# Message passing over edges: operands of the second loop's products moved from SBUF to PSUM

## What is computed

```
e0 = feat0[edge_src];  e1 = feat1[edge_src]
ea0 = edge_attr[:, :1];  ea1 = edge_attr[:, 1:4]
h = gelu(edge_scalar_attr @ W_mlp1 / sqrt(8));  h = gelu(h @ W_mlp2 / sqrt(64))
w00, w01, w10, w11 = h @ Wp_00, h @ Wp_01, h @ Wp_10, h @ Wp_11
out0_a = w00 * e0 * ea0
out0_b = w11 * sum(e1 * ea1, over 3 components) / sqrt(3)
out1_a = (w01 * e0) x ea1          # 32 x 3
out1_b = w10 * e1 * ea0            # 32 x 3
n0, n1 = segment_sum of [out0_a, out0_b], [out1_a, out1_b] by edge_dst
```

## Time and profile before

| | us |
|---|---|
| time, median of 3 runs | 5811.78 (5809.79 to 5824.05) |
| the profiled execution's own time | 5874.45 |
| its span from first to last instruction | 5872.5 |
| busy in the span: PE / DVE / ACT / POOL | 3935.2 / 3079.9 / 1722.9 / 3442.4 |
| mean granted TensorE clock, share of full speed | 0.796 |

### The profile page before, as it was taken

The page is one execution under the profiler, slowest core; times in us unless marked ns, Lnnn a source line. Parts: engine busy times, 40 slices in busy tenths (PEclk is TensorE's granted clock), DMA queues, the critical chain, the costliest instruction groups (busy, mean ns, idle before and its releaser), DMA issues. The chain is left out here.

```text
span 5872.5 us, 85330 instructions
## 1 busy us (share of the span) xinstructions
PE 3935.2 (67%) x14958; PEld 2602.4 (44%) x14958; DVE 3079.9 (52%) x9402; ACT 1722.9 (29%) x5039; POOL 3442.4 (59%) x3340
## 2 busy tenths in 40 slices
PE   5566666667666666666675777767677676686667
PEld 3233434444333434334453554445455454454445
DVE  3333443444433444434595666666676565675566
ACT  1233333333333333333531222222222121222222
POOL 3455555555555555555275577667677676666663
PEclk6777778877877778877897787878888787887788
DMA  5333433333333333333212111111111111111111
GB/s 162 103 103 101 106 105 102 105 103 104 103 101 99 104 100 105 102 102 106 60 34 62 40 44 43 42 43 44 44 42 43 42 43 42 43 42 42 43 43 38
DMA packets 395187, 430.87 MB, mean 73 GB/s; under 512 B 194933, under 2 KB 286713, under 8 KB 394763
## 3 DMA queue, kind: packets, MB, share of 16 engines
q0 software_dynamic: 103168, 211.49, 13.8%
q1 hardware_dynamic: 290294, 214.04, 13.6%
q10 hardware_dynamic: 1428, 2.71, 0.2%
HBM read 411.12 MB, written 16.78 MB: 73 GB/s over the span
## 5 line engine op out<-in xcount | busy, mean ns | idle before, releaser
L1105 POOL DMA_INDIRECT conv_rows<-feat,conv_idx x1612 | 1780.2, 1104 | 892.7 <-issue 545.1
L160 POOL DMA_INDIRECT ring_rows<-xl,ring_idx x1612 | 1524.8, 946 | 1323.8 <-DVE attn_msg L730 750.8
L589 PE MATMUL attn_sums_ps<-attn_msg,attn_onehot 128*128 128x136 f32 x3224 | 584.4, 337 | 857.3 <-ACT attn_onehot L630 402.5
L1121 PE MATMUL conv_sums_ps<-conv_vals,conv_onehot 128*128 128x256 f32 x3224 | 932.7, 439 | 146.8 <-issue 80.3
L589 PEld LDWEIGHTS attn_sums_ps<-attn_msg,attn_onehot 128*128 128x128 f32 x3224 | 515.7, 236 | 899.6 <-issue 461.2
L1128 PE MATMUL conv_w_ps<-c_Wp,conv_hid 128*128 128x256 f32 x1612 | 508.5, 445 | 548.2 <-ACT conv_hid L1158 278.2
L1152 ACT ACTIVATE conv_scaled<-conv_w_ps,conv_edge 128x64 f32<-128x64 f32 x1612 | 374.7, 315 | 1701.9 <-remote 804.5
L1121 PEld LDWEIGHTS conv_sums_ps<-conv_vals,conv_onehot 128*128 128x128 f32 x3224 | 660.8, 216 | 407.6 <-issue 295.3
L736 DVE TENSOR_TENSOR attn_leaky<-attn_pre_ps,attn_fifth 128x512 f32<-128x512 f32 x403 | 276.9, 687 | 979.4 <-issue 498.5
L623 ACT ACTIVATE attn_fifth<-attn_pre_ps 128x512 f32<-128x512 f32 x403 | 238.4, 592 | 1620.2 <-remote 1110.5
L1128 PEld LDWEIGHTS conv_w_ps<-c_Wp,conv_hid 128*128 128x128 f32 x1612 | 350.5, 224 | 648.4 <-ACT conv_hid L1158 302.6
(11 more groups left out here) (169 smaller groups left out, 4674.7 us busy)
## 6 DMA issues: line engine op xcount, KB each, us to landing
c_xT<-in_attrT SPq DMA_DIRECT2D x403, 256.0 KB
attn_rel<-rel_group SPq DMA_DIRECT2D x403, 126.0 KB
ring_rows<-xl,ring_idx POOLq DMA_INDIRECT x1612
conv_rows<-feat,conv_idx POOLq DMA_INDIRECT x1612
conv_radial<-in_radialT SPq DMA_DIRECT2D x806, 8.0 KB
attn_xr_win<-xr_parts SPq DMA_DIRECT2D x403, 31.5 KB
attn_limit<-limit SPq DMA_DIRECT2D x403, 16.0 KB
conv_idx<-in_src_tiles SPq DMA_DIRECT2D x403, 2.0 KB
```

Source lines behind the costliest of these rows:

```text
L160: pool.indirect_dma_start(self.rows[:, b, t, :], None, self.q["xl"][:, :], bass.IndirectOffsetOnAxis(ap=self.idx[:, s.slot(2), j * TG + t: ...
L589: last = nc.tensor.matmul(to, onehot[:, g.slot(2), t, :], msg[:, g.slot(2), t, :, :].rearrange("p h o -> p (h o)"), start=wins > 1 or t == ...
L1105: pool.indirect_dma_start(rows[:, k.slot(NX), t, :], None, q["feat"][:, :], bass.IndirectOffsetOnAxis(ap=idx[b][:, t:t + 1], axis=0)).then ...
L1121: last = nc.tensor.matmul(to, onehot[:, g.slot(2), t, :], vals[:, g.slot(2), t, :], start=wins > 1 or t == 0, stop=wins > 1 or t == TG - 1)
```

## The change

`scaled` is gone: ACT writes the scaled weights over the weights in `w_ps`, in PSUM. The componentwise products `dots` lie in a bank of PSUM. The three components of the edge's vector are copied by ACT, for each group, to `edge3` in PSUM (12 elements per partition, one buffer), behind a wait for `vals_ready` of the group before, and DVE waits for that copy. One `reduce_sum` over the three components takes the place of two additions. Every DVE operation of the eight (now seven) thus reads at most one tensor from SBUF.

```diff
-        scaled = tile("scaled", [P, 2, TG, 2 * MUL])
-        dots = tile("dots", [P, TG, 3, MUL])
-        dot = tile("dot", [P, 2, TG, MUL])
+        dot = tile("dot", [P, TG, MUL])
...
+        dots = bank("dots_ps", [P, TG, 3, MUL])
+        edge3 = bank("edge3_ps", [P, TG, 3])
+        edge3_ready = sem("edge3_ready")
...
-        PRODUCTS = 5
+        PRODUCTS = 4
...
                     act.wait_ge(w_ready, g.uses())
-                    at_least(act, vals_ready, g.back(2).uses())
                     for t in range(TG):
-                        nc.scalar.activation(scaled[:, g.slot(2), t, :], w_ps[:, g.slot(2), t, 0:2 * MUL], ACT.Copy,
+                        here = w_ps[:, g.slot(2), t, 0:2 * MUL]
+                        nc.scalar.activation(here, here, ACT.Copy,
                                              scale=edge4[:, bass.ds(g.index(TG, t), 1), 0:1].rearrange("p t c -> p (t c)")).then_inc(scaled_ready, 1)
+                    at_least(act, vals_ready, g.back(1).uses())
+                    nc.scalar.activation(edge3[:, :, :], edge4[:, bass.ds(g.index(TG), TG), 1:4], ACT.Copy).then_inc(edge3_ready, 1)
...
-                        a1 = bc(edge4[:, bass.ds(g.index(TG), TG), 1:4], 3, MUL)
+                        a1 = bc(edge3[:, :, :], 3, MUL)
                         to, w = vals[:, s, :, :], w_ps[:, s, :, :]
                         at_least(dve, vals_ready, g.back(1).uses())
+                        dve.wait_ge(edge3_ready, g.uses())
                         dve.wait_ge(rows_gathered[g.slot(NX)], g.uses(NX, 16 * TG))
                         nc.vector.tensor_tensor(dots[:, :, :, :], e1, a1, ALU.mult).then_inc(products, 1)
                         dve.wait_ge(scaled_ready, g.uses(1, TG))
                         nc.vector.tensor_tensor(scal[:, :, :], w[:, :, 2 * MUL:3 * MUL], e0, ALU.mult).then_inc(products, 1)
+                        nc.vector.tensor_tensor(to[:, :, 0:MUL], w[:, :, 0:MUL], e0, ALU.mult)
                         dve.wait_ge(products, g.index(PRODUCTS, 1))
-                        nc.vector.tensor_tensor(dot[:, 0, :, :], dots[:, :, 0, :], dots[:, :, 1, :], ALU.add).then_inc(products, 1)
-                        nc.vector.tensor_tensor(to[:, :, 0:MUL], scaled[:, s, :, 0:MUL], e0, ALU.mult)
+                        nc.vector.reduce_sum(dot[:, :, :], dots[:, :, :, :].rearrange("p t c w -> p t w c"), mybir.AxisListType.X).then_inc(products, 1)
+                        nc.vector.tensor_tensor(to[:, :, MUL:D].rearrange("p t (c w) -> p t c w", c=3), e1, bc(w[:, :, MUL:2 * MUL], 2, 3), ALU.mult)
+                        dve.wait_ge(products, g.index(PRODUCTS, 2))
+                        nc.vector.tensor_tensor(to[:, :, D:D + V3].rearrange("p t (c w) -> p t c w", c=3), bc(scal[:, :, :], 2, 3), a1, ALU.mult).then_inc(products, 1)
                         dve.wait_ge(products, g.index(PRODUCTS, 3))
-                        nc.vector.tensor_tensor(dot[:, 1, :, :], dot[:, 0, :, :], dots[:, :, 2, :], ALU.add).then_inc(products, 1)
-                        nc.vector.tensor_tensor(to[:, :, MUL:D].rearrange("p t (c w) -> p t c w", c=3), e1, bc(scaled[:, s, :, MUL:2 * MUL], 2, 3), ALU.mult)
-                        nc.vector.tensor_tensor(to[:, :, D:D + V3].rearrange("p t (c w) -> p t c w", c=3), bc(scal[:, :, :], 2, 3), a1, ALU.mult).then_inc(products, 1)
-                        dve.wait_ge(products, g.index(PRODUCTS, 4))
-                        nc.vector.tensor_tensor(to[:, :, D + V3:DX], dot[:, 1, :, :], w[:, :, 3 * MUL:4 * MUL], ALU.mult).then_inc(vals_ready, 1)
+                        nc.vector.tensor_tensor(to[:, :, D + V3:DX], dot[:, :, :], w[:, :, 3 * MUL:4 * MUL], ALU.mult).then_inc(vals_ready, 1)
```

## The result

| | median of its runs | lowest to highest | profiled execution | mean clock granted there |
|---|---|---|---|---|
| before | 5829.51 us (6 runs) | 5809.79 to 5843.61 | 5874.45 us | 0.796 |
| after | 5944.26 us (6 runs) | 5932.32 to 5966.89 | 5959.12 us | 0.791 |

The change makes the kernel 2.0% slower: ratio 1.0203, 95% interval 1.0177 to 1.0229. The forecast of no change (5812 us, with 5700 to 5920 as its own range) missed. The time lies where the rival "the first loop's rhythm" put it (5902 to 5982, about 5940 us, with a chance of 0.19), and inside the wide range of 5500 to 5990.

The account below looks back on a forecast made before the run. The second loop's pace was put at 6.56 us per group, with held-up gathers and POOL's pauses trading off rather than POOL's work binding. Gathers, DVE and ACT each added 0: 5874 us profiled, 5812 by the median, range 5500 to 5990.

Parts of the forecast that it names:

- The forecast of no change: Whole kernel: freed held-up time returns as POOL pauses, so 5812 us, own range 5700 to 5920, chance 0.52.
- the first loop's rhythm: Rival, second loop: without held-up gathers, pauses rise to 1.8 to 2.0 us per group; about 5940 us, chance 0.19.
- Gathers are held up by reads of two SBUF tensors: Second loop: gathers stand still while DVE reads two SBUF tensors, 0.64 us per group, 258 us at most.
- What takes their place: Second loop: POOL's pauses grow by the 0.64 us freed, keeping held-up time plus pauses at 1.58 us per group.
- POOL's idle time: Ahead of second-loop gathers: a rise of about 250 us would be the sign of the forecast.
- Windows: Second loop: the forecast fails if windows of 316 us hold more than 205 or fewer than 183 gathers.
- Quick stretches: Second loop: stretches at 4 us per group would be gone, a sign listed for the forecast.
- VectorE: Second loop: two additions go, one reduction comes, +0.07 us per group; +28 us if DVE were the bound, counted as nothing.
- Operands in PSUM: DVE's second-loop operations: 2 to 8 ns on six operations, 5 to 20 us in 403 groups, counted as nothing.
- ACT's copy: Second loop: 12-element copy and its wait, 0.2 us per group, hidden behind other work; up to +242 us if uncovered.

Follow-up runs that it names:

- e6: Kernel after with one useless 384-element product more per group on VectorE, reading two SBUF tensors: 5930.86 us, 1.019 of the kernel before.
- e3: Kernel after with the edge vector copied to PSUM only once, without later copies and their waits: 5936.69 us, 1.019 of the kernel before.
- e4: Kernel after with each second-loop group's four gathers replaced by one plain transfer of 512 contiguous rows: 4823.78 us, 0.825 of the kernel before.
- e1: Kernel after with a 128-element memset behind each second-loop gather, POOL's sequencer waiting at group start for the previous group's memsets: 5725.00 us.
- e2: Kernel after with a 512-element memset behind each second-loop gather and the same wait as e1: 6248.99 us, 1.071 of the kernel before.
- e5: Kernel before with e1's 128-element memsets behind each second-loop gather: 5762.49 us, 0.990 of the kernel before.
- e8: Kernel after with e1's memsets and wait in both loops: 5346.64 us, 0.918 of the kernel before.
- e9: As e1, with 120-element memsets in eight groups' places, so the sequencer waits only for memsets of eight groups before: 5925.39 us.
- e10: Kernel after with one 8-element memset per second-loop group, behind its last gather, awaited by POOL's sequencer at the next group's start: 5691.81 us.
- e11: Kernel after with e10's single memset and wait in both loops: 5567.07 us, 0.955 of the kernel before.
- e12: As e8, but the sequencer waits for the previous group's third memset, not the fourth; neighbouring groups write different places: 5897.02 us.
- e7: Kernel after with three semaphore increments, awaited by nobody, behind each second-loop gather: 5882.70 us, 1.009 of the kernel before.

## Why the prediction failed, step by step

**Gathers are held up by reads of two SBUF tensors: right.** 947 ns, with none above 1.2 us, after the change; 266 of the 1612 were above it before. This is where the Trainium skill's rule ("SBUF — State Buffer", section "Who interferes with whom") agrees with the trace.

**What takes their place: the step that failed.** I let the pauses grow by just what was freed, to keep the sum at 1.58 us per group. They grew by 0.86 instead of 0.64, and the sum is 1.80. The row for it was on the table: the first loop, where nothing is held up, has 1.8 to 2.0. I took the second loop's own sum as nearest, though it was made of two parts of which the change removes one. The other loop, which was already in the state that the change brings about, was the nearer row. The price of that rival, about 5940 us, was right, and to within 4 us by luck. It stood on 5812 us, where six runs give 5829.51, and the rise was 115 us in the 90 to 170 it allowed. Of the 132 us between forecast and measurement, 89 are the pauses, 18 the base, and 26 stay unexplained. The forecast's own range would have held pauses of 1.80 us.

**POOL's idle time** rose by 339 us, not 250. **Windows**: 185 to 189 gathers, inside the 183 to 205 that I allowed; bounds this wide could not have shown the miss. **Quick stretches**: the fastest eight groups in a row take 37.4 us after the change, 32.0 before. Behind one another at under 4.2 us came up to 12 groups before; now it is six once, and otherwise one or two. So the stretches are all but gone, while single groups at that pace remain: 103 of 402 come within 4.1 us of the one before (137 in the kernel before).

**VectorE: right.** The reduction takes 550 ns (0.47 from start to start was the estimate, 0.55 the expected reading), VectorE's busy time rose from 3079.9 to 3097.8 us, and e6 shows that 222 us more cost nothing.

**Operands in PSUM: right.** Line 1210 (one operand in PSUM) takes 286 ns and line 1211 283, as in the earlier trace rows 284 and 282. The prediction counts four operands newly read from PSUM; there are five (lines 1208, 1211, 1213, 1214 and 1216). Of the 384-element ones, 1214 and 1216 take 548 and 551 ns, and 1208, which also writes PSUM, 557; their counterparts before take 548. The 65 ns more that the Trainium skill gives for PSUM ("VectorE: DVE Perf Modes", section on the TRN2 errata) do not show in these rows.

**ACT's copy: right in its price.** It takes 198 ns (0.2 us was the estimate), and without copy and wait the kernel takes 8 us less, within the scatter (e3). It is not always hidden, though: of VectorE's idle time ahead of line 1208, 134.4 us are ended by it. They cost nothing, since e3 is no faster without it.

**What stays open.** That the kernel before was faster because held-up gathers let signals through is not shown. e6 tried it and brought back only a tenth of the held-up time; a kernel with the edge vector alone in SBUF was not run. Nor is it shown that lateness explains the 2%: from the end of PE's weights to ACT's scaling pass 2.21 us per group before and 2.24 after, in the mean of all 403, though before, the scaling waits for values as well. More than 1 us passes in 113 groups before and in 179 after, so the late starts came in fewer and longer spells. Why the pauses came out at 1.80 us and not at 1.58 is thus open. So is by which way gathers delay signals between other engines. The runs show only with what the delays come and go in the second loop: none without gathers (e4), none where memsets part the gathers and the sequencer waits for its engine once a group (e1, e2, e5, e8). Memsets without that wait leave signals late (e9), so does the wait without them (e10, e11), and so does a wait one memset earlier (e12). The time gains with the full wait, late signals or not. Why e7's increments gave 62 us was not followed.

## What to carry to other kernels

Where one engine issues many indirect DMAs back to back and other engines wait on signals that are "remote" or on nothing at all, try making its sequencer wait once in each step for its own engine, with a small operation behind each gather: in both loops it cost 725 us of added POOL work here and gave 8%. When a change removes a stall, look for a loop in the same kernel that never had it, and take its pace as the forecast. Freeing an engine that is not the bound can lengthen the kernel: here 254 us came off POOL and 115 came onto the time.

## What the hardware showed that was not expected

- POOL's sequencer ran ahead of its engine: a gather handed over every 0.71 us, taken every 1.25.
- ACT started 0.14 us after PE's matmul where memsets parted the gathers and POOL's sequencer waited for its engine once a group (e1), 2.56 us after it in the kernel after, and 6.58 with the wait alone (e10).
- Adding 373 us of memsets to POOL in one loop made the kernel 219 us shorter, but only together with the wait. Nearly the same memsets without it gave 19 us, and the wait without them 252.
- The same wait one memset earlier, with the memsets in two places by turns, turned 5347 into 5897 us.
